# Attention and expert layer on one core: scores of two heads on TensorE's row halves, with a new order of steps

## The reference

```python
x = x + attention(layernorm(x))      # 16 heads of 16 channels, rotary q and k, causal softmax, output projection Wo
x = x + experts(layernorm(x))        # 8 experts, top 2 of them per token, capacity 153 slots per sequence and expert
# attention: scores = q k^T / sqrt(16), masked above the diagonal; out = softmax(scores) v
# experts:   o = silu((x Wfc + b) * (x Wgate + b)) Wproj + b, weighted by the softmax of the two chosen logits
```

## Time and profile before

| | |
|---|---|
| median of 3 runs | 1405.36 us (1402.96 to 1407.62) |
| the profiled execution | 1391.76 us, of it the span of the instructions 1389.9 us |
| busy, share of the span | PE 89%, PE weight loads 74%, DVE 52%, ACT 36%, POOL 50% |
| granted TensorE clock, mean | 0.943 of full speed |
| DMA | 147.86 MB, mean 106 GB/s |

### The profile page before, as it was taken

The page is one execution under the profiler, slowest core; times in us unless marked ns, Lnnn a source line. Parts: engine busy times, 40 slices in busy tenths (PEclk is TensorE's granted clock), DMA queues, the critical chain, the costliest instruction groups (busy, mean ns, idle before and its releaser), DMA issues.

```text
span 1389.9 us, 25801 instructions
## 1 busy us (share of the span) xinstructions
PE 1238.5 (89%) x8360; PEld 1023.6 (74%) x8360; DVE 729.6 (52%) x1512; ACT 496.3 (36%) x988; POOL 697.0 (50%) x984
## 2 busy tenths in 40 slices
PE   3699999999898989988899999999999999997830
PEld 3465656566565656548899999999999999997730
DVE  5777776858676767556333343343333433333336
ACT  2145444535353535454223332333233332332100
POOL 4334243343425251267755665576656764634445
PEclk9699999999999999999999999999999999998865
DMA  5766545444434453432312211131122112102247
GB/s 138 216 208 193 177 115 144 109 132 103 138 93 139 100 149 93 137 124 60 96 62 91 70 62 62 64 98 54 66 78 87 54 58 70 64 28 72 69 131 249
DMA packets 82333, 147.86 MB, mean 106 GB/s; under 512 B 9263, under 2 KB 59832, under 8 KB 78142
## 3 DMA queue, kind: packets, MB, share of 16 engines
q1 hardware_dynamic: 64576, 111.37, 28.1%
q0 software_dynamic: 7936, 26.60, 5.6%
q10 hardware_dynamic: 9728, 8.67, 2.0%
HBM read 93.05 MB, written 53.61 MB: 106 GB/s over the span
## 4 chain that ended last, share of the span: by engine, by line
PE 45%; another core or an unknown queue 2%; DVE 1%; POOL 1%; issue 1%; DMA 0%; DVEq 0%; ACT 0%; POOLq 0%; ACTq 0%
PE ps L77 44%; PE ps L1264 1%; DVE raw L1427 1%; POOL wg_hi L1544 1%; POOL wf_hi L1544 0%; DMA wg_hi<-slot_outputs,slot_all 0%; DVE al L1417 0%; DVEq L1454 0%; DVE ah L1408 0%; POOLq L1572 0%; ACT hid L1349 0%; ACT fc L1360 0%; DVE xl L1332 0%; DVE gated L1455 0%
## 5 line engine op out<-in xcount | busy, mean ns | idle before, releaser
L1491 POOL TENSOR_TENSOR al<-hid,ah 128x384 fp32r<-128x384 f32 (+1 forms) x176 | 187.4, 1065 | 232.9 <-DVE ah L1408 232.9
L1360 ACT ACTIVATE fc<-ps,b_fc 128x384 f32<-128x384 f32 (+1 forms) x192 | 115.5, 602 | 482.4 <-PE ps L77 441.2
L1455 DVE SCALAR_TENSOR_TENSOR gated<-ps,b_gate,fc 128x384 f32<-128x384 f32 (+1 forms) x192 | 123.4, 643 | 268.1 <-PE ps L77 220.2
L794 DVE TENSOR_REDUCE mx<-ps 128x2 f32<-128x256 f32 (+3 forms) x256 | 206.6, 818 | 67.1 <-PE ps L408 56.5
L577 ACT ACTIVATE probs<-ps 128x512 f32<-128x512 f32 (+1 forms) x256 | 125.6, 541 | 73.8 <-PE ps L434 72.0
L408 PE MATMUL ps<-kst,qst 65*128 65x256 f32 (+2 forms) x512 | 151.7, 380 | 0.0
L1442 DVE TENSOR_TENSOR o_sb<-ps,b_proj 128x256 f32<-128x256 f32 x80 | 33.9, 424 | 179.0 <-PE ps L77 175.1
L569 ACT ACTIVATE probs<-ps 128x256 f32<-128x256 f32 (+1 forms) x128 | 62.6, 490 | 164.4 <-PE ps L425 150.0
L445 PE MATMUL ps<-probs,v_sb 128*32 128x512 f32 (+3 forms) x1024 | 98.8, 459 | 14.2 <-DVE v_sb L822 14.0
L77 PE MATMUL ps<-xh,wg_hi 128*128 128x384 f32 (+1 forms) x384 | 104.4, 353 | 5.0 <-DVE gated L1455 4.2
L935 POOL TENSOR_TENSOR rope_c<-qk_b,rope_table 128x512 f32<-128x512 f32 x32 | 42.7, 1333 | 128.9 <-ACT qk_b L605 128.7
(11 more groups left out here) (181 smaller groups left out, 2577.5 us busy)
## 6 DMA issues: line engine op xcount, KB each, us to landing
qk_parts<-hilo SPq DMA_DIRECT2D x32, 512.0 KB, 3.1
qst<-qk_parts SPq DMA_DIRECT2D x64, 256.0 KB, 4.8
kst<-qk_parts SPq DMA_DIRECT2D x64, 256.0 KB, 5.2
slot_tokens<-zeros POOLq DMA_DIRECT2D x12, 816.0 KB, 5.6
rows<-slot_tokens SPq DMA_DIRECT2D x24, 384.0 KB, 3.7
slot_outputs<-o_sb SPq DMA_DIRECT2D x72, 128.0 KB
raw<-in_wf SPq DMA_DIRECT2D x8, 1024.0 KB, 6.1
raw<-in_wg SPq DMA_DIRECT2D x8, 1024.0 KB, 7.6
```

What stands on the lines that cost most here:

```text
L794: V.reduce_max(mx[:, g % 2, i, 2 * pr:2 * pr + 2], both[:, :, 0:P * (i + 1)], AXX)\
L1360: A(fc[:, hc % 2, 0:width], ps[:, FC + hc % 2, 0:width], ACT.Identity, bias=b_fc[:, e, hc:hc + 1]).then_inc(fc_out, 1)
L1455: V.scalar_tensor_tensor(gated[:, hc % 2, 0:width], ps[:, GATE + hc % 2, 0:width], b_gate[:, e, hc:hc + 1], fc[:, hc % 2, 0:width], ALU.ad ...
L1491: G.tensor_tensor(al[:, at, 0:width], hid[:, hc % 2, 0:width], ah[:, at, 0:width].bitcast(F32), ALU.subtract).then_inc(al_done, 1)
```

## The change

**Score stacks.** q and k rows of a head are 48 instead of 64: [q high, q low, q high] against [k high, k high, k low]; row 48 carries the maximum. The heads of a pair lie on rows 0 to 48 and 64 to 112 of the array, into two banks. The mask is made of two products of 64 rows, one per half; `load_stack` issues 8 DMAs for 768 KB per group, and `send_max` two DMAs, in step 3.

```diff
-            def pass1(b, g, u):
...
+            rows_of = [slice(HALF * hh, HALF * (hh + 1)) for hh in range(2)]
+            def first(b, g, u):
...
+                for hh, half in enumerate(rows_of):
+                    mm(first_bank(u, hh)[:, bass.ts(i, P)], pick_bf[half, 0], causal_bf[half],
+                       start=True, stop=False, skip_group_check=True)
...
+                for hh in range(2):
+                    rows = slice(HALF * hh, HALF * hh + MROW)
+                    last = mm(first_bank(u, hh)[:, 0:width], qst[rows, g, pr, bass.ts(i, P)], kst[rows, g, pr, 0:width],
                               start=False, stop=True, skip_group_check=True)
                 last.then_inc(p1_done, 1)
...
+            def second(t, g, u):
                 j, pr = u // 2, u % 2
                 if u == 0:
+                    wait(pe, ld_max, 32 * (t + 1))
+                wait(pe, exp_done, TILES2 * t + u)
                 q0 = min(P * j, T - 2 * P)
+                for hh, half in enumerate(rows_of):
+                    mm(ps[:, S2 + hh, P * j - q0:P * (j + 1) - q0], pick_bf[half, 1], later_bf[half],
                        start=True, stop=False, skip_group_check=True)
                 for hh in range(2):
+                    rows = slice(HALF * hh, HALF * hh + ROWS)
+                    last = mm(ps[:, S2 + hh, 0:T - q0], kst[rows, g, pr, bass.ts(j, P)], qst[rows, g, pr, q0:T],
+                              start=False, stop=True, skip_group_check=True)
+                last.then_inc(p2_done, 1)
```

```diff
+                elif kind == "P":
+                    wait(pe, exp_done, TILES2 * (s - 2))
...
+                    for j in range(TT):
+                        for h in range(GH):
+                            last = mm(misc[32 * h:32 * h + 32, P * j:T], v_sb[:, j, GH * group + h, :],
+                                      probs[:, (g + 1) % 2, h, PROB_AT[j]:PROB_AT[j + 1]], start=(j == 0), stop=(j == TT - 1))
+                    last.then_inc(pv_done, 1)
```

```diff
+            (0, 0): (("X", 0, LOW), ("X", 1, HIGH)),
+            (0, 1): (("P", 0, LOW),), (0, 2): (("M", 0, HIGH),), (0, 3): (("A", 0, LOW),), (0, 4): (("Q", 0, HIGH),),
+            (0, 5): (("H", 0, LOW),), (0, 6): (("Q", 1, HIGH),), (0, 7): (("H", 1, LOW),),
+            (1, 0): (("Q", 2, HIGH),),
+            (1, 1): (("P", 0, LOW),), (1, 2): (("M", 0, HIGH),), (1, 3): (("A", 0, LOW),), (1, 4): (("L", 0, HIGH),),
+            (1, 5): (("Q", 3, LOW),), (1, 6): (("R", 0, HIGH),),
+            (2, 1): (("P", 0, LOW),), (2, 2): (("M", 0, HIGH),), (2, 3): (("A", 0, LOW), ("F", 0, HIGH)),
+            (2, 5): (("T", 0, LOW),), (2, 6): (("T", 1, HIGH),),
+            (3, 0): (("O", 0, LOW), ("O", 1, HIGH)),
+            (3, 1): (("P", 0, LOW),), (3, 2): (("M", 0, HIGH),), (3, 3): (("A", 0, LOW),), (3, 4): (("V", 0, HIGH),),
+            (3, 5): (("V", 1, LOW),),
```

At the start, the normalisations, cosine products and Newton chains of sequences 0 and 1 run one after another on POOL, and PE waits before its first scores for the two V evictions and the folded bias:

```diff
+            pe.wait_ge(v_out, 2)
+            pe.wait_ge(bo_out, 1)
             body(0)
```

More of the change, by code:

```diff
@@ L380, in _ @@
             body(1)
-            with sp.Fori(2, 7) as b:
+            with sp.Fori(2, 6) as b:
                 body(b)
-            body(7)
-            body(8)
+            for b in range(6, 9):
+                body(b)
             rt["late_slot"]["sp"] = body_slot
@@ L541, in _ @@
-            pe.wait_ge(ld_const, 16)
-            for g, u in FIRST:
-                if PIECES[g, u][0] != "X":
-                    pe.wait_ge(w_split, {("Q", 0): 1, ("Q", 1): 2, ("Q", 2): 1, ("Q", 3): 2}.get(PIECES[g, u], 3))
-                piece(-1, g, u)
-            pe.wait_ge(ld_w, 16 * 10)
+                    if there(b, 0, 7):
+                        first(b, g, u)
+                    if second_there(s):
+                        second(s - 2, (g - 2) % 4, u)
+                    pieces(b, g, u)
@@ new lines, in _ @@
+            pe.wait_ge(ld_const, 16)
+            for at in range(len(ORDER)):
+                kind, n = ORDER[at][2:4]
+                if (kind, n) in FIRST:
+                    if kind != "X":
+                        pe.wait_ge(w_split, {("Q", 0): 1, ("Q", 1): 2, ("Q", 2): 1, ("Q", 3): 2}.get((kind, n), 3))
+                    piece(-1, at)
+            pe.wait_ge(ld_w, 16 * 11)
+            pe.wait_ge(bv_ready, 1)
+            for c in range(CK):
+                last = mm(bank_of(-1, "X", 1)[:, 0:C], bv_wide[:, c, :], wo[:, c, :], start=(c == 0), stop=(c == CK - 1))
@@ L547, in _ @@
+            last.then_inc(bo_done, 1)
             pe.wait_ge(made, 5)
             pe.wait_ge(ld_ones, 32)
+            pe.wait_ge(v_out, 2)
+            pe.wait_ge(bo_out, 1)
             body(0)
             body(1)
-            with pe.Fori(2, 7) as b:
+            with pe.Fori(2, 6) as b:
                 body(b)
-            body(7)
-            body(8)
-            rt["late_slot"]["pe"] = piece
+            for b in range(6, 9):
+                body(b)
+            rt["late_slot"]["pe"] = pieces
@@ L776, in body_slot @@
-                if (g, u) in ((3, 2), (3, 3)) and piece_there(b, g, "O"):
-                    n = u - 2
-                    wait(dve, o_done, 2 * b - 2 + n + 1)
+                    for n in range(CK):
+                        wait(dve, xT_out, 2 * b + 2 + n + 1)
+                        V.tensor_tensor(xnT[1][:, n, :], bank_of(b, "X", n), xnT[0][:, n, :].bitcast(F32), ALU.subtract)\
+                            .then_inc(xl_out, 1)
+                if (g, u) == (3, 1) and there(b, 1, 8):
                     wait(dve, xr_done, b)
@@ L992, in _ @@
             pool.wait_ge(st_zero, 16 * FILLS)
-            with pool.Fori(2, 7) as b:
+            with pool.Fori(2, 6) as b:
                 body(b)
-            body(7)
-            body(8)
+            for b in range(6, 9):
+                body(b)
             rt["late_slot"]["pool"] = body_slot
```

610 lines of the change are left out of this document (285 added, 325 removed), and 7 rows, old and new, of the table PIECES.

## The result

The kernel after takes **1495.08 us** (median of 4 runs, 1490.83 to 1497.75), the kernel before beside it 1404.16: a ratio of 1.064, with a 95% interval of 1.061 to 1.068. It is slower by 91 us, where the prediction said 55 us faster.

A forecast was written before the change was run, and what follows sets the result against it. PE was taken to bound the attention loop; an iteration would fall from 73.7 to 63.9 us (57.2 + 4.2 + 2.5), with the other bodies and ends -55 in all, giving 1350 us, range 1305 to 1394.

The forecast's parts named there:

- the slack named: SP's queue: stores of q, k and maxima leave in step 3 and have 5 steps, over 8 us, to land.
- rival 3: Attention loop on PE: row halves don't overlap, 75 us per iteration against 73.7, +19, 1424 us; chance 0.10.
- some 6 us: +1.6: Body 0: X of sequence 1 moves to step (0, 0), so PE waits some 6 us for POOL's normalisation; net +1.6 us.
- between 0.2 and 0.64: Attention loop: time in us of each of eight normalisations that POOL gains per iteration.
- The experts: 0 (-1 to +3): Experts' part after attention: the change costs 0 us, between -1 and +3.
- 57.2 of streaming: Attention loop: PE streams 57.2 us per iteration, from 65.8 less 4 x 2.6 for overlapping pairs plus 1.8 for switches.
- 4.2 of waits for the banks: Attention loop: `second` uses both banks and PE waits for the previous step's exponential; 4.2 us per iteration (0 to 6).
- 2.5 for DVE: Attention loop: lumps of DVE work, mainly reductions and routing, cost PE 2.5 us per iteration (0 to 6).
- 54 if a switch is free: Attention loop: PE's streaming per iteration, in us, if changing the array's shape cost nothing instead of 0.09 a switch.
- body 8 (+6): Last body: only two groups have `second`, exponential rounds set the pace and the last P is exposed; +6 us.
- Rival 4, the clock: Attention loop: PE, waiting in small pieces, is granted 1.2 GHz more often; 1375 to 1395 us; 0.15 together with rival 2.
- rival 2: Attention loop: a shape switch costs 0.24 us instead of 0.09, gain gone, 1395 to 1405; 0.15 together with Rival 4, the clock.

The follow-up runs named there:

- a_spread: Kernel after with each 16-row part of a score stack loaded by its own DMA, 12 per group instead of 8, same bytes: 1397.05 us, ratio 1.044 to the kernel before.
- after_third: Kernel after, unchanged, measured again in the fifth set: 1459.8 us, +119 against the kernel before (1.090).
- b_narrow: Kernel before with the stacks' q rows in the kernel after's order (slowest dimension 2) and k in two DMAs: 1438.14 us, +98.5 (1.075).
- after_xr: Kernel after with only POOL's sum of xr and the output bias moved to step (2, 1) from (0, 2): 1442.46 us, +104.5 against the kernel before (1.079).
- combo4_act: combo3b with ACT's high parts and small router exponential placed behind the exponentials PE waits for: 1376.64 us, -21 against the kernel before (0.986).
- combo3b: combo1 plus x_in of sequence 2 loaded ahead of stacks of groups 2 and 3, statistics in step (1, 5), after_late's order: 1344.33 us, 1.006 to kernel before.
- norm_dve: Kernel after with both normalisations back on DVE, in steps (3, 6) and (3, 7): 1453.91 us, +114 against the kernel before.
- spread_xr: Kernel after with 16-row stack loads and the sum of xr in step (2, 1), normalisations still on POOL: 1428.51 us, +43 against the kernel before.
- after_late: Kernel after with only DVE's and POOL's order beside the first expert changed (slots before residual sum, Newton right behind scatters): 1457.6 us, +120 against the kernel before.
- best_again: combo4_act, unchanged, measured again in the fifth set: 1314.64 us, -26 against the kernel before (0.982).
- combo1: Kernel after with 16-row stack loads, both normalisations on DVE and the sum of xr in step (2, 1): 1371.05 us, +31 against the kernel before (1.026).
- before_again: Kernel before, unchanged, run for its profile in the fourth set: 1397.4 us.

## Why the prediction was wrong, step by step

**The step that failed** is one sentence: "SP issues 8 stack DMAs per group instead of 4, in sum 768 KB instead of 1024 ... I cost these at nothing; their cover is the slack named". It counted instructions and bytes, and not the shape of the access. The narrow loads run at 49 GB/s, the load issued behind each of them at the start holds SP's queue for 1.7 to 4.5 us, and what follows comes late: the stacks and maxima (46 us of PE's waits, 12.0 before), x_in at the start, and in every body xr (landing in 10.6 us, 4.2 in a_spread). So the slack was gone, and the wait was where the prediction had put it for that case, in step 0 of a group. This term, put at nothing, costs about 60 us (a_spread against after_third, in two sets), and such loads alone make the kernel before 98.5 us slower (b_narrow). None of the rivals had them; rival 3, the slower one, had a mechanism that the first timeline refuted.

**Queues behind a wait.** The "some 6 us: +1.6" of body 0 looked at PE's wait for POOL's normalisation, which measures 1.0 us, and not at `input_stats` in step (0, 4), a new wait of DVE for x_in with the reductions queued behind it: PE waited 33.8 us there. The sum of xr, moved from (2, 1) to (0, 2) right behind the issue of its load, was not costed at all (about 15 us in after_xr). Nor was ACT's order in steps where `large_part` waits for DVE: in combo4_act, turning it takes the kernel from 0.6% above the kernel before (combo3b) to 1.4% below, in different sets.

**Normalisation on POOL, "between 0.2 and 0.64"**: 1.22 us, twice the upper end. The estimate went by elements alone, with the cosine product as its base. It cost little while POOL waited anyway (norm_dve), and 3.7 us of PE's time an iteration in spread_xr.

**"The experts: 0 (-1 to +3)"**: +13, from the order in which POOL and DVE finish the last sequence, of which 8 are won back by after_late.

**What held.** The iteration was forecast at 63.9 us: 57.2 of streaming, 4.2 of waits for the banks, 2.5 for DVE. best_again measures 62.8 to 64.4, and in the one shown PE is busy for 57.6. That the sum fits is in part luck: the waits for DVE are 5.5 us (term 2.5, too low), those for exponentials 0.6 (term 4.2, too high; combo1, with ACT's old order, has 4.2), and the two errors cancel. The pairs take 0.24, 0.30 and 0.35 us (forecast 0.29 to 0.40), a switch 0.1 (0.09). The bound "54 if a switch is free" doesn't follow from its own terms (57.2 less 52 x 0.09 is 52.5); nothing else rests on it. Against the bodies of the first trace, the start (+2.5) is +2.6 and body 0 (+1.6) is +1.0; body 1 gains 5.2 instead of 7.7 and body 7 5.5 instead of 8, and body 8 (+6) comes out at +10.9 up to the experts.

**Rival 4, the clock**, was right as a mechanism and put too low (0.15 for it and rival 2 together). In the kernel after the waits shown go with products at 1.2 GHz, and the clock of the iteration shown is 0.83; in combo3b it is 0.50 for some 10 us behind the seven waits. In the main it follows the waits: with them mended it rose from 0.83 to 0.93 (combo3b) and 0.95 (best_again). But the kernel before, unchanged, has iterations at 0.91 and at 1.00, so it is not shown that waits alone set it.

**The size of the gain, -55**, took 73.7 us as what an iteration of before costs. The same kernel has one of 70.6 us at a clock of 1.00 (before_again), so part of the 9.8 us per iteration is the clock of one execution. The mended schedule wins 21 and 26 us in two sets, not 55. Up to the experts best_again is 51.6 us shorter than the first trace, but no trace shows the kernel before in the fifth set. An estimate: it is 51 us faster there than in that trace, of which 27 lie in the experts if they take what they take in b_narrow (736.4 against 763.5 us), so 24 would lie in the attention, and some 28 us are left as the gain there.

## What to carry to other kernels

When a change rewrites a DMA, compare the order of its dimensions and the DMA share of a window, not only bytes and counts: a slowest dimension of 2 made a load eight times narrower and cost more than the whole rearrangement gained. When a step moves, ask for each engine what stands behind its new wait in the same queue, and place what TensorE waits for ahead of what only waits itself. If a predicted gain is missing while no engine is busier, the mechanism may still be sound: mend the waits one by one before giving it up.

## What the runs showed that I had not expected

- **Two heads on row halves take little more than one**: at 2.4 GHz the two products of 512 columns and their two masks take 0.35 us from start to start, where one product of 512 columns takes 0.23.
- **POOL seems to pay for scalars taken from memory**: with two per-partition scalars an instruction of 128x256 takes 1.22 us; the split of expert weights (L1522), of the same shape and also with two operations, but with constants, takes 0.41 to 0.50 in the kernel before. That the scalars make the difference is an inference from these rows; no run tests it.
- **A large POOL operation stops a small one of DVE.** Timeline of POOL and DVE in combo3b:

```profile
334.33 2.37 POOL L935 TENSOR_TENSOR xr<-xr,bo_all 128x1024 f32<-128x1024 f32 x1
...
334.52 2.23 DVE L704 TENSOR_TENSOR eq<-logits,top 128x32 f32<-128x32 f32 x1
```

  The comparison of 32 elements, 0.19 us when alone, ends with POOL's sum, at 336.7. A reduction from PSUM beside a POOL product (at 331.98 us) keeps its 1.2 us. The Trainium skill (GPSIMD Engine Reference, Specifications) names contention with DVE instructions that have two SBUF inputs; the trace agrees.
- **The same kernel differs by 5% between sets** (1338 to 1404 us), with a mean clock of single executions between 0.92 and 0.97. Of the experts' part, the first nine tenths of PE's products take the same time in the first trace of the kernel before and in b_narrow of the first set (620.7 and 621.3 us). The 27 us lie in what follows: there PE waits 17.0 us at a stretch for an operand of its last products (`al`) in the trace of the kernel before, and 2.8 in b_narrow. Only ratios within a set could be used.

Left open: what makes the sets differ; how much of best_again's 5.5 us of waits for DVE could go by spreading the routing; and the exact share of each mended part, since they hide one another.
